# A language-model layer stack on one core: statistics turned by every fourth token, inverse roots read without a stride

## The reference

```python
for i in range(N_LAYERS):                       # 4 layers, width 128
    h = _ln(x, cms_ln_g[i], cms_ln_b[i])        # (x - mean) * rsqrt(var + eps) * g + b
    h = gelu(einsum('bsd,df->bsf', h, cms_W1[i]) + cms_b1[i])
    x = x + einsum('bsf,fd->bsd', h, cms_W2[i]) + cms_b2[i]
```

## Time and profile before

| | |
|---|---|
| median of 3 runs | 435.57 us (431.88 to 436.09) |
| the profiled execution's own time | 436.5 us |
| its span in the trace | 434.7 us |
| busy share of the span | PE 91%, DVE 83%, ACT 76%, POOL 64%; PEld 73% |
| granted TensorE clock, mean | 0.973 of full speed |

### The profile page before, as it was taken

How to read it: one execution, slowest core, us unless ns; L and a number is a source line. 1 busy time by engine, 2 the same in 40 slices (tenths; PEclk the granted TensorE clock), 3 DMA queues, 4 the chain that set the end, 5 groups by cost and what they waited for, 6 DMA issues and landing times.

```text
span 434.7 us, 6335 instructions
## 1 busy us (share of the span) xinstructions
PE 397.2 (91%) x2000; PEld 318.3 (73%) x2000; DVE 359.2 (83%) x809; ACT 329.2 (76%) x557; POOL 277.3 (64%) x436
## 2 busy tenths in 40 slices
PE   4788789999999999999999998988877998999996
PEld 2576478888778877778888897777665766877884
DVE  3898588988899888988899877978775779989773
ACT  1263688999889988788887744766865988989994
POOL 0556587777877789678779554686533676435543
PEclk9898899999999999999999988999998999999998
DMA  6800012222222221312212000000000000000001
GB/s 211 324 2 0 1 27 47 32 44 49 50 38 37 49 50 27 67 32 48 45 35 44 1 0 2 1 3 2 0 0 2 1 1 14 12 14 12 14 12 25
DMA packets 15833, 14.94 MB, mean 34 GB/s; under 512 B 9780, under 2 KB 10552, under 8 KB 15544
## 3 DMA queue, kind: packets, MB, share of 16 engines
q1 hardware_dynamic: 15800, 14.54, 13.6%
HBM read 13.42 MB, written 1.11 MB: 33 GB/s over the span
## 4 chain that ended last, share of the span: by engine, by line
PE 42%; DVE 25%; ACT 20%; POOL 5%; issue 4%; DMA 2%; SPq 0%; POOLq 0%; DVEq 0%; ACTq 0%
PE ps L1427 38%; DVE hid_lo L1008 5%; ACT hid L670 5%; ACT hid_hi L675 4%; DVE stats L934 4%; DVE xn L998 4%; ACT xn_hi L666 3%; PE ps L1448 2%; ACT ezf L791 2%; ACT hid L854 2%; ACT w_all L860 2%; DVE hh L1216 1%; PE ps L1456 1%; DMA rstd_row<-roots 1%; DMA xn<-in_w_f 1%
## 5 line engine op out<-in xcount | busy, mean ns | idle before, releaser
L670 ACT ACTIVATE hid<-ps,b_fold 128x512 f32<-128x512 f32 x128 | 84.2, 682 | 18.1 <-PE ps L1427 18.0
L1008 DVE TENSOR_TENSOR hid_lo<-hid,hid_hi 128x1024 fp32r<-128x1024 f32 x64 | 78.4, 1225 | 17.6 <-ACT hid_hi L675 17.3
L1427 PE MATMUL ps<-xn_hi,w_all 128*128 128x512 f32 x256 | 89.0, 409 | 3.8 <-DVE xn_lo L1003 3.8
L1427 PE MATMUL ps<-hid_hi,w_all 128*128 128x512 f32 x256 | 84.9, 393 | 0.0
L675 ACT ACTIVATE hid_hi<-hid 128x1024 fp32r<-128x1024 f32 x64 | 67.9, 1061 | 2.0
L1427 PEld LDWEIGHTS ps<-xn_hi,w_all 128*128 128x128 f32 x256 | 48.7, 190 | 16.9 <-DVE xn_lo L1003 4.0
L1427 PEld LDWEIGHTS ps<-hid_hi,w_all 128*128 128x128 f32 x256 | 48.1, 188 | 9.9
L1427 PE MATMUL ps<-xn_lo,w_all 128*128 128x512 f32 x128 | 50.6, 395 | 0.0
L1427 PE MATMUL ps<-hid_lo,w_all 128*128 128x512 f32 x128 | 49.8, 389 | 0.0
L472 POOL TENSOR_TENSOR var_in<-stats 128x4 f32<-128x4 f32 x30 | 28.0, 932 | 30.2 <-DVE stats L934 30.2
L854 ACT ACTIVATE hid<-ps,eb_fold 128x512 f32<-128x512 f32 x64 | 44.1, 689 | 1.6 <-PE ps L1427 1.2
(11 more groups left out here) (228 smaller groups left out, 903.5 us busy)
## 6 DMA issues: line engine op xcount, KB each, us to landing
rstd_row<-roots SPq DMA_DIRECT2D x29, 256.0 KB, 3.9
hh<-in_tokens SPq DMA_DIRECT2D x8, 256.0 KB, 7.9
hid<-in_w SPq DMA_DIRECT2D x1, 1024.0 KB, 7.3
rstd_row<-in_w SPq DMA_DIRECT2D x1, 1024.0 KB, 10.3
out<-hh SPq DMA_DIRECT2D x8, 128.0 KB, 2.0
ew_raw<-in_expert_w SPq DMA_DIRECT2D x1, 512.0 KB, 9.7
roots<-rstd SPq DMA_DIRECT2D x29, 2.0 KB, 1.4
ew_raw<-in_expert_w SPq DMA_DIRECT2D x1, 256.0 KB, 9.9
```

Source lines behind the costliest of these rows:

```text
L670: act.activation(hid[:, j % 2, f, :], bank[f], ACT.Gelu, bias=b1_fold[:, j // B * F + f:j // B * F + f + 1]).then_inc(gelu_done, 1)
L1008: dve.tensor_tensor(hid_lo[:, j % 2, 2 * p:2 * p + 2, :], hid[:, j % 2, 2 * p:2 * p + 2, :], hid_hi[:, j % 2, 2 * p:2 * p + 2, :].bitcast( ...
L1427: return pe.matmul(out, lhsT, rhs, start=start, stop=stop)
```

## The change

The 29 turns of steps 3 to 31 take every fourth token instead of 128 neighbours: transpose t reads tokens 4 q + t for q = 0 to 127, so its weight load reads `x` with a step of four elements (16 bytes). Statistics and roots are then made as before, but partition q now holds tokens 4 q to 4 q + 3, and the store puts the root of token n at place n. Line 998 therefore reads `rstd_row` from end to end. The turns of the first layer norm and of steps 0 to 2, the store, the load, and the operations with their order and waits on every engine are the same in both programs.

```diff
             def norm_x(j):
                 ...
                 else:
                     dve.wait_ge(rstd_loaded, (j - SPREAD_BY_PE + 1) * 16)
-                    by_tile = rstd_row[:, j % 4, :].rearrange("p (q t) -> p t q", t=NT)
-                    dve.tensor_tensor(tiles(xn[:, j % 2, :], P), tiles(x[:, j % B, :], P), by_tile,
-                                      ALU.mult).then_inc(normed, 1)
+                    dve.tensor_tensor(xn[:, j % 2, :], x[:, j % B, :], rstd_row[:, j % 4, :], ALU.mult).then_inc(normed, 1)
...
-            def turn(src, ready, count, n):
+            def turn(src, ready, count, n, every_fourth=False):
 
                 pe.wait_ge(ready, count)
                 pe.wait_ge(stats_ready, n + FREE)
+                fourths = src.rearrange("p (q t) -> p t q", t=NT)
                 for t in range(NT):
-                    last = pe.transpose(bank[TB][:, t * P:(t + 1) * P], src[:, t * P:(t + 1) * P], ident)
+                    part = fourths[:, t, :] if every_fourth else src[:, t * P:(t + 1) * P]
+                    last = pe.transpose(bank[TB][:, t * P:(t + 1) * P], part, ident)
                 last.then_inc(x_t, 1)
...
             for j in range(L * B):
                 if 0 < j and j + 3 < B:
-                    turn(x[:, j + 3, :], x0_ready, j + 4, place_ffn(j + 3))
+                    turn(x[:, j + 3, :], x0_ready, j + 4, place_ffn(j + 3), every_fourth=True)
                 elif B <= j + 3 and j + 3 < L * B:
-                    turn(x[:, (j + 3) % B, :], x_ready, j + (4 - B), place_ffn(j + 3))
+                    turn(x[:, (j + 3) % B, :], x_ready, j + (4 - B), place_ffn(j + 3), every_fourth=True)
                 up(j)
                 ...
                 if j == 0:
                     centre_w1(2)
-                    turn(x[:, 3, :], x0_ready, 4, place_ffn(3))
+                    turn(x[:, 3, :], x0_ready, 4, place_ffn(3), every_fourth=True)
                     centre_w1(3)
```

## The result

The changed kernel takes 429.24 us in the median of four runs (427.52 to 430.44), the kernel before 435.44 (431.88 to 436.09). The ratio is 0.9893, with a 95% interval of 0.9847 to 0.9939: 1.1% faster, between 0.6 and 1.5%. The forecast was 431.5 us, with a range of 429.5 to 438.5.

What follows compares the result with a forecast made beforehand. The VectorE and ScalarE chain was taken as the bound, TensorE 0.07 us behind. Of 5.8 us of waits, 0.9 and 0.8 stay, turns cost nothing: 4.1 us gained, 435.57 - 4.1 = 431.5 us, range 429.5 to 438.5 (8 in 10).

Steps and rivals of the forecast that it cites:

- What bounds the kernel: Steps 3 to 28: the VectorE and ScalarE chain, 5.97 us a step, is the bound; TensorE stands 0.07 behind.
- The multiply: Line 998 without its 16-byte step falls from 1081 to 684 ns, 0.40 us less on VectorE in each step.
- What becomes late next: After the faster multiply TensorE is the bound in quiet steps, VectorE 0.38 us ahead; 4.1 us gained in sum.
- 5.8 to be had at most: All of TensorE's waiting in steps 3 to 28, 5.8 us, the most that any VectorE gain can give there.
- TensorE's floor: The time TensorE could do a step in without waiting: 5.97 - 0.07 = 5.90 us.
- The step after the largest pieces of weight preparation: VectorE pieces of 0.60 us make it late by 0.22 at four places, so 0.9 us of waiting stays.
- Step 21: Its multiply waits for roots delayed by GpSimd's memset, whatever VectorE does; 0.8 us of waiting stays.
- The turns: TensorE's transpose weight loads with a 16-byte step cost nothing extra (lower end) to 0.10 us each; lower end taken.
- rival 1: Stepped loads become the bound: 0.10 us more each gives 437.8 us, slower from 0.07; chance 0.16 for 0.07 to 0.13.
- 79 d: Cost on TensorE's path if each stepped load is longer by d: three uncovered loads a turn; at most 7.9 us.
- rival 4: TensorE's stepped loads cost a partly paid price, 0.01 to 0.07 us each: 432 to 435.5 us; chance 0.12.
- Steps 29 to 31: VectorE waits for hid_hi after its multiply anyway, so a shorter multiply only lengthens that wait; no gain.

Runs made afterwards that it cites:

- The multiply alone: Against the kernel before: turns unchanged, the multiply reads the roots from end to end without a step; ratio to before 0.9893 (0.9852 to 0.9934).
- turns-only kernel: Against the changed kernel: turns still take every fourth token, the multiply again reads the roots with its 16-byte step; ratio to before 0.9977 (0.9947 to 1.0006).

## Why the prediction was right, and where not

**What bounds the kernel.** Right. The chain of VectorE and ScalarE ended last, 5.97 us a step, with TensorE's own 5.92 just behind. The multiply alone moved the whole chain to TensorE; put back in the turns-only kernel it undid all of it; doubled, it made the step 6.17, as long as the loop.

**The multiply.** 684 ns was predicted, 671 measured.

**What becomes late next.** TensorE, as predicted, and the gain of the stretch was predicted as 4.1 us and is 4.43. But that the sum came so close is luck: four of its terms were off by 0.5 us or more each, two one way and two the other. In the runs it reads: 5.8 to be had at most, 0.86 of which the multiply alone doesn't get either (154.28 - 149.31 = 4.97), less 0.54 for the dearer loads, is 4.4. Term by term:

- TensorE's floor was put at 5.90 and is 5.92 with plain loads (the multiply alone). Over 25 steps that is 0.5 us less to be had than the 5.8. The 0.07 of waiting at the turn was read right and did come back (0.63 to 0.56 from the turn's first load to the next step's), but the 24 products between one turn and the next take some 0.02 longer than before, 5.36 instead of 5.34 us from a step's first load to the turn's; why, I can't say.
- The step after the largest pieces of weight preparation was to keep 0.22 us. It keeps nearly nothing: 24 steps of 5.95 and step 27, whose eight head products make it 6.89, are 149.7 us, and the stretch took 149.85. VectorE is ahead by 0.55 in a quiet step instead of the 0.38 that was worked out, so a piece of 0.60 makes it late by about 0.05, and the step that starts at 149.80, in which such a piece follows the hid_lo at 150.13, takes 6.00 instead of 5.95. What was wrong is mostly TensorE's step: at 5.95 instead of 5.90 the next step's load comes 0.05 later after VectorE is ready, and the hid_lo that VectorE starts from lies 0.05 less behind the load. ScalarE's shift, taken as 0.15 from a range of 0.08 to 0.2, is 0.18: hid_lo's second half started 154.60 - 148.13 = 6.47 after the first load of its step, and now starts 150.13 - 143.84 = 6.29 after it. Since the prediction had 6.50 for the 6.47, counting the 0.02 of issue twice, that makes another 0.06. With plain loads (the multiply alone), where TensorE leaves less room, three of these steps take 6.01 to 6.03 and keep 0.1 each.

```profile
150.13 1.23 DVE L1006 TENSOR_TENSOR hid_lo<-hid,hid_hi 128x1024 fp32r<-128x1024 f32 x1 [0.93 <-ACT hid_hi L675]
```

- Step 21 was to keep 0.8 us for its late roots, and keeps nothing. GpSimd had been taken as a clock that VectorE doesn't touch: "This moves with the roots, not with VectorE". Its timeline behind the same memset, before and after:

```profile
165.01 1.66 POOL L472 TENSOR_TENSOR var_in<-stats 128x4 f32<-128x4 f32 x1
...
167.19 1.25 POOL L476 TENSOR_TENSOR var_in<-var_in 128x4 f32<-128x4 f32 x1
...
170.22 0.63 POOL L482 TENSOR_TENSOR rstd<-var_in,two 128x4 f32<-128x4 f32 x1
```

```profile
160.14 0.63 POOL L472 TENSOR_TENSOR var_in<-stats 128x4 f32<-128x4 f32 x1
...
161.73 0.20 POOL L476 TENSOR_TENSOR var_in<-var_in 128x4 f32<-128x4 f32 x1
...
164.24 0.20 POOL L482 TENSOR_TENSOR rstd<-var_in,two 128x4 f32<-128x4 f32 x1
```

The memset starts 1.7 us after the first load of step 18 in both kernels, but the root is done 10.19 us after that load before (170.85 - 160.66) and 8.64 in the changed kernel (164.44 - 155.80): 1.55 earlier, where 1.03 was missing. The 128x4 subtraction takes 0.2 us when VectorE is elsewhere and up to 1.7 when it has a two-input operation in work: before, line 472 ends at 166.67, just behind VectorE's xn_lo at 166.61, and line 476 at 168.44, just behind hid_lo at 168.39. So VectorE's schedule does move the roots. That the multiply is what changed it is shown by the halves: with the slow multiply and stepped turns the root comes after 10.17 us and the wait is back, at 0.59; with the fast multiply and plain turns it comes after 8.65 and no multiply of the stretch waits for its roots. That it goes by way of these collisions is read from the rows and wasn't tried by itself.

**The turns.** The forecast had no price, d = 0, and that was wrong, by a little: the loads lengthened, which the prediction had itself named as a sign of being wrong. Its other reading of that sign, that "a longer load at once decides for rival 1", was wrong too: rival 1 goes by the delay and needed 0.07, and a load can be 0.065 longer and delay what follows by only 0.012. The price d was bounded by 0 and 0.10 us; it is 0.011 to 0.012 for each load, four loads a step, 0.03 to 0.05 with the first partly hidden. At 79 d that is 0.9 us, and 0.54 was measured on the path. So the case that came is, by its mechanism, the low end of rival 4, a partly paid price with d between 0.01 and 0.07, which had a chance of 0.12; in the total it was outweighed by the two terms above that were too dark. The reason given for the low end, that a plain load moves a column only every 0.85 ns, fits what was found, though no run isolates it: the pace hardly changed, while the record of one load grew from 139 to 204 ns. Anyone who had put the longer record into the sum, 0.065 for each load, would have expected 79 x 0.065 = 5.1 us of loss. The rule on lines of 16 bytes that the prediction cited for the first rival (the Trainium skill, "SBUF — State Buffer", Specifications (TRN2): full bandwidth wants at least two hits on a line) does not describe these loads: 8 bytes, with two columns on each line, cost no less than 16. On VectorE only the 16-byte step was seen.

**Steps 29 to 31.** That "a shorter multiply only makes this wait longer" was wrong by 0.19 us in the other direction: with VectorE in another rhythm, one GpSimd subtraction came to stand just ahead of hid_lo, which took 0.16 and 0.14 longer in steps 29 and 30. It comes with the multiply and not with the turns: steps 28 to 30 take 19.29 us with the multiply alone and 19.11 with the turns alone.

**The rest.** About 1.8 us of the profile's 6.0 (2.87 - 1.11) lie ahead of and behind the steps that the change bears on, most of it with the clock, and the medians differ by more than the 4.2 us for that reason or by the spread of the runs. The ratio's interval, 2.7 to 6.7 us of gain, holds both.

## What to carry to other kernels

Where the busiest engine is busy for 99% of a stretch, look at the first instruction that needs another engine's result: if it starts right behind that result every time (here 0.05 us), the bound is elsewhere, and what can be gained is the busiest engine's waits, not the other engine's saving (here 4.4 of 10 us). A permutation that costs one engine a stepped read was cheapest here where reads overlap: on the path 0.03 us a quiet step in TensorE's weight loads, 0.2 in VectorE's multiply (4.97 us over 25 steps, for 0.41 a step of VectorE's time), 5 in a store of 4-byte pieces.

## What the runs showed of the hardware

- A weight load of 128 fp32 columns for a transpose takes 139 ns without a step and 202 to 209 with one of 8 or 16 bytes, but the next load starts 0.11 and 0.12 us after it.
- A GpSimd operation of 128x4 elements (line 476) takes 0.20 us alone and 1.25 beside VectorE's operations with two SBUF inputs, ending 0.05 us after VectorE's. Line 472, which runs beside the multiply, went from 960 to 578 ns with it. It also works the other way: VectorE's hid_lo took 1.39 instead of 1.23 behind a GpSimd subtraction that had started first and ran 0.31 us into it, and 1.53 behind one that ran 0.45 into it. This is what the Trainium skill, "SBUF — State Buffer", "SBUF: two separate sides", says of the port pair that the two share: whoever starts first has it for its whole instruction. The traces agree in the order; VectorE's record grew by about 0.15 us less than the overlap in both cases.
- A store of 2 KB takes 1.4 us from issue to landing in 128 pieces of 16 bytes, and 10.6 in 512 pieces of 4 (medians).
